# Two-stage cross attention: the first pair's v taken from row totals that VectorE turns and a DMA moves, in place of four small products of TensorE

## The chip, the core and the metric

The kernel runs on one core of one Trainium2 chip. The metric is the device time of one execution in microseconds; the time given for a kernel is the median of its runs.

## What is computed

```python
# stage one: x (16, 256, 512), ctx (16, 256, 512)
q = einsum('blh,oh->blo', x, w_q)
k = einsum('bsh,oh->bso', ctx, w_k)
v = einsum('bsh,oh->bso', ctx, w_v)
probs = softmax(einsum('blh,bsh->bls', q, k) / sqrt(512))
x = x + alpha * einsum('blh,oh->blo', einsum('bls,bsh->blh', probs, v), w_o)
# stage two: x (16, 256, 512) as (b, c, n), x_2 = ctx as (b, c, n)
g_x     = (g_w @ x_2 + g_b).transpose(0, 2, 1)
theta_x = (theta_w @ x + theta_b).transpose(0, 2, 1)
phi_x   = phi_w @ x_2 + phi_b
y = ((theta_x @ phi_x) / 512 @ g_x).transpose(0, 2, 1)
wy = w_w @ y + w_b
out = bn_gamma * (wy - bn_mean) * rsqrt(bn_var + 1e-5) + bn_beta + x
```

Stage two has no softmax, so the kernel multiplies in another order. It needs, for each batch, phi_x times the transposed context. The bias g_b enters through one number for each of the 128 inner channels: the sum of phi_x over its 512 columns. That vector of 128 numbers for each batch is what the kernel calls `v`. It equals phi_w times the row totals of the context (256 totals for each batch) plus 512 times phi_b.

## The kernel before

The 16 batches go in 8 pairs. `pair(0, first=True)` is written out, pairs 1 to 6 are a loop on every engine, pair 7 is written out again. In front of pair 0 stands a setup: it multiplies the weights (w_k with w_q into `qk`, w_v with w_o into `ov`, g_w with w_w into `wg`), and makes the first tiles of the first pair.

Every float32 factor is split into a high and a low half (`_hi`, made by ScalarE in the helper `hi`, L634; `_lo`, made by VectorE in the helper `lo`, L892). A product of float32 tiles is then three products of TensorE: `product`, L363 to L370. The order of the work is written out by hand on each engine, and semaphores join the engines. SyncE issues most of the DMAs, ScalarE's queue a few.

Names that the change and the prediction speak of:

- `c_sums` (L656): ScalarE runs over `c_raw`, the context of a pair, and leaves the row totals in `c_sum`: partition p, one column for each batch and each of its two row tiles. It costs four activations with an accumulator for each pair.
- `send_sums` (L663) and `fetch_sums` (L668): both issued by ScalarE. The first stores `c_sum` to the DRAM tensor `sums_moved`, two values (8 bytes) for each partition and batch. The second reads it back, broadcast to all 128 partitions, into columns of the tile `row` (`sum_rows`).
- `weigh_sums` (L998) on VectorE multiplies `sum_rows` by `phi_rows` (phi_w, one row for each partition), and `v_sums` (L768) on ScalarE adds each row up into `v`. Pairs 1 to 7 get their `v` in this way; the store and the fetch stand in the pair ahead.
- `first_v` (L449): pair 0 gets its `v` from TensorE. ScalarE makes the high half of the totals (`sum_sides`, L703), VectorE the low half (L976), TensorE multiplies phi_w by them in four products with a moving side of 4 or 2 columns, and VectorE adds two columns and the bias (L1167, L1169).
- `t1_rows` (L1082) on VectorE uses `v`; its result goes into `t1`, and TensorE waits for `t1_made` ahead of `gram_rows(1, 0)` in pair 0.
- `gram_rows` (L436), `gram_squares`, `gram_close`, `gram_part`: context times transposed context; its lower blocks travel through DRAM. `phi_gram` (L445) multiplies phi_w by it; in pair 0 TensorE waits there for `gram_lo`.
- `theta_rows` (L491) waits for the low half of x1 (`x1_lo`), and `delta` for the low half of `vo` and of `pT`.

```python
            def first_v():
                pe.wait_ge(sums_lo, 1)
                for k in range(KS):
                    pe.matmul(bank[FIRST_V_BANK][:, 0:4], phi_w[0][:, k], sum_sides[:, k].rearrange("p h b -> p (h b)"),
                              start=(k == 0), stop=False)
```

## Time and profile before

| | |
|---|---|
| time, median of 3 runs | 388.9 us (388.58 to 389.62) |
| time of the profiled execution | 388.78 us |
| span of the profiled execution | 386.8 us |
| granted clock of TensorE over the span | 0.999 |
| instructions | 5571 |
| VectorE busy | 310.8 us, 80% |
| ScalarE busy | 206.0 us, 53% |
| packets of ScalarE's DMA queue (q10) | 3632, 2.77 MB, 2.5% of the 16 engines' span |
| share of TensorE in the chain that ended last | 97% |

The span is the time from the first to the last instruction on the core; the device time of the same execution is 1.98 us longer. TensorE's matmuls overlap in the records: each of 512 columns is shown with some 0.39 us, while one starts every 0.23 us. So a wait of TensorE is read from the starts in a timeline, and not from its busy time alone.

### The profile page before, as it was taken

The numbers are of one execution on the slowest core, as the hardware profiler recorded it, in microseconds if no ns is written. First come the engines' busy times: TensorE is split into PE (matmuls) and PEld (weight loads), VectorE is DVE, ScalarE is ACT, GpSimd is POOL, SyncE is SP. The second block draws the span as 40 slices with busy tenths as digits, with TensorE's granted clock in tenths as the row PEclk, the third lists the DMA queues.
The fourth block names the chain that finished last, engine by engine and source line by source line (L and its number), as shares of the span: only waits on it lengthen the run. The fifth ranks groups of instructions, "written<-read, shape, count | busy, mean of one in ns | idle before, by whom it ended". The sixth has DMA issues, their size and how long they took to land.

```text
span 386.8 us, 5571 instructions
## 1 busy us (share of the span) xinstructions
PE 381.8 (99%) x1783; PEld 319.5 (83%) x1783; DVE 310.8 (80%) x590; ACT 206.0 (53%) x440; POOL 0.4 (0%) x5
## 2 busy tenths in 40 slices
PE   8999999999999999999999999999999999999995
PEld 5888888888888888888888888888888888888885
DVE  5899778887699777986798967986788876986786
ACT  4477668433664267543665258452665347552553
POOL 0000000000000000000000000000000000000000
PEclk9999999999999999999999999999999999999999
DMA  8985741476386646856356655865496664044423
GB/s 248 379 319 198 266 128 54 150 283 233 110 212 193 240 139 214 166 190 216 107 178 206 216 169 177 217 186 192 122 204 177 211 190 136 19 117 153 145 83 108
DMA packets 59563, 70.11 MB, mean 181 GB/s; under 512 B 6688, under 2 KB 49568, under 8 KB 56480
## 3 DMA queue, kind: packets, MB, share of 16 engines
q1 hardware_dynamic: 55920, 67.20, 56.0%
q10 hardware_dynamic: 3632, 2.77, 2.5%
q8 instruction: 6, 0.10, 0.1%
q14 instruction: 5, 0.04, 0.0%
HBM read 51.06 MB, written 18.89 MB: 181 GB/s over the span
## 4 chain that ended last, share of the span: by engine, by line
PE 97%; DMA 1%; DVE 1%; ACT 0%; issue 0%; SPq 0%
PE bank L367 24%; PE bank L368 23%; PE bank L369 23%; PE bank L421 8%; PE bank L440 7%; PE bank L407 5%; PE bank L429 4%; PE bank L472 2%; PE bank L476 1%; DMA xb<-w_k 1%; DVE xb L1152 0%; DVE xb L1147 0%; PE bank L393 0%; ACT theta_hi L634 0%; ACT t_sides L634 0%
## 5 line engine op out<-in xcount | busy, mean ns | idle before, releaser
L367 PE MATMUL bank<-ov_hi,c_sides 128*128 128x512 f32 x128 | 50.0, 391 | 0.0
L368 PE MATMUL bank<-c_sides,qk_hi 128*128 128x512 f32 x128 | 49.9, 390 | 0.0
L369 PE MATMUL bank<-c_sides,qk_lo 128*128 128x512 f32 x128 | 49.9, 390 | 0.0
L368 PE MATMUL bank<-ov_lo,c_sides 128*128 128x512 f32 x128 | 49.9, 390 | 0.0
L367 PE MATMUL bank<-c_sides,qk_hi 128*128 128x512 f32 x128 | 49.8, 389 | 0.0
L369 PE MATMUL bank<-ov_hi,c_sides 128*128 128x512 f32 x128 | 49.8, 389 | 0.0
L634 ACT ACTIVATE t_sides<-bank 128x512 fp32r<-128x512 f32 x32 | 19.0, 593 | 36.9 <-PE bank L369 36.9
L421 PE MATMUL bank<-t_sides,xT_hi 128*128 128x512 f32 x128 | 31.9, 391 | 0.0
L634 ACT ACTIVATE probs<-bank 128x512 f32<-128x512 f32 x16 | 9.4, 586 | 37.9 <-PE bank L429 37.9
L892 DVE TENSOR_TENSOR t_sides<-bank,t_sides 128x512 fp32r<-128x512 f32 x32 | 22.0, 687 | 8.5 <-ACT t_sides L634 8.5
L634 ACT ACTIVATE x_hi<-xb 128x512 fp32r<-128x512 f32 x32 | 19.9, 630 | 16.4 <-DVE xb L1072 16.2
L369 PEld LDWEIGHTS bank<-ov_hi,c_sides 128*128 128x128 f32 x128 | 24.0, 188 | 5.1
L369 PEld LDWEIGHTS bank<-c_sides,qk_lo 128*128 128x128 f32 x128 | 24.0, 188 | 5.1
L367 PEld LDWEIGHTS bank<-ov_hi,c_sides 128*128 128x128 f32 x128 | 24.1, 188 | 4.8
L368 PEld LDWEIGHTS bank<-c_sides,qk_hi 128*128 128x128 f32 x128 | 24.0, 188 | 4.8
L367 PEld LDWEIGHTS bank<-c_sides,qk_hi 128*128 128x128 f32 x128 | 24.0, 188 | 4.8
L368 PEld LDWEIGHTS bank<-ov_lo,c_sides 128*128 128x128 f32 x128 | 24.1, 188 | 4.7
L440 PE MATMUL bank<-c_sides 128*128 128x384 f32 (+1 forms) x128 | 27.4, 364 | 0.0
L421 PEld LDWEIGHTS bank<-t_sides,xT_hi 128*128 128x128 f32 x128 | 23.5, 188 | 4.5
L440 PEld LDWEIGHTS bank<-c_sides 128*128 128x128 f32 x128 | 23.5, 188 | 3.1
L367 PE MATMUL bank<-vo_hi,pT_hi 128*128 128x512 f32 x64 | 25.0, 391 | 0.0
L737 ACT ACTIVATE probs<-probs,neg_max 128x256 f32<-128x256 f32 x32 | 16.0, 502 | 16.7 <-DVE neg_max L1020 16.7
(157 smaller groups left out, 815.4 us busy)
## 6 DMA issues: line engine op xcount, KB each, us to landing
cT_raw<-ctx_t SPq DMA_DIRECT2D x8, 1024.0 KB, 8.0
xT_raw<-x_t SPq DMA_DIRECT2D x8, 1024.0 KB, 5.1
c_raw<-ctx_n SPq DMA_DIRECT2D x8, 1024.0 KB, 8.1
xb<-x SPq DMA_DIRECT2D x16, 512.0 KB, 4.1
out<-xb SPq DMA_DIRECT2D x14, 512.0 KB, 2.8
gram_moved<-gram_blocks SPq DMA_DIRECT2D x16, 256.0 KB, 2.7
gram_blocks<-gram_moved SPq DMA_DIRECT2D x64, 64.0 KB, 1.9
moved<-blocks SPq DMA_DIRECT2D x16, 256.0 KB, 2.3
```

The lines of the kernel that those rows point to most:

```text
L367: pe.matmul(dst, ahi, bhi, start=(k == 0), stop=False)
L368: pe.matmul(dst, ahi, blo, start=False, stop=False)
L369: mm = pe.matmul(dst, alo, bhi, start=False, stop=(k == k_tiles - 1))
L407: mm = pe.matmul(bank[KH * n + m][:], lhs[a][:, k, tile(m)], rhs[b][:, k, :], start=(k == 0 and a == b), stop=(k == KH - 1 and a == 1))
L421: mm = pe.matmul(banks[:, SCORE_BANK[b]][:, lt], xT[0][:, b, k, tile(lt)], t_sides[:, k, b].rearrange("p h s -> p (h s)"), start=(k == 0), ...
L429: mm = pe.matmul(banks[:, SCORE_BANK[b]][:, lt, 0:S], xT[1][:, b, k, tile(lt)], tT[0][:, k, b], start=False, stop=(stop and k == KH - 1))
L440: mm = pe.matmul(bank[GRAM_BANK[b][i]][:, i * P:], cT[0][:, k, b, tile(i)], c_sides[:, k, b].rearrange("p h s -> p (h s)")[:, i * P:], sta ...
L472: pe.matmul(banks[:, t1_banks][:, n], u[0][:, 2 * b + k], wg_sides[:, k].rearrange("p h l -> p (h l)"), start=(k == 0), stop=False)
L476: mm = pe.matmul(banks[:, t1_banks][:, n, 0:L], u[1][:, 2 * b + k], wg[0][:, k], start=False, stop=(k == KS - 1))
L634: act.activation(dst, src, ACT.Identity, **more).then_inc(made, 1)
L737: e = act.activation(probs[:, b, lt], probs[:, b, lt], ACT.Exp, bias=neg_max[:, b, lt:lt + 1], scale=SCALE, accum_out=row_sum[:, b, lt:lt ...
L892: dve.tensor_tensor(parts[1][at], src, parts[0][at].bitcast(F32), ALU.subtract).then_inc(made, 1)
```

## The change

1. `first_v`, the two halves of `sum_sides`, `phi_h` and the two additions that opened its bank are gone.
2. `c_sum` becomes a tile of 128 x 32, cleared once by GpSimd. VectorE transposes it in 32 x 32 blocks into `c_sum_blocks` (`turn_sums`), once in the setup and once in each of the pairs 0 to 6. `send_sums` stores that tile, 128 bytes from each partition; `fetch_sums` reads 4 runs of 512 bytes for each partition, where it read one of 2048. `phi_n` has its columns in the new order, and `weigh_sums` and `v_sums` walk over four pieces of 64 columns.
3. In the setup ScalarE now issues a store of the first pair's totals and a fetch of them. In pair 0 VectorE's `weigh_sums` and ScalarE's `v_sums` are added.
4. In pair 0 `send_sums` stands behind `x1_part(0, .)`; in the loop it stands where it stood, and waits for `sums_turned`.
5. TensorE no longer waits for `v_made` in pair 0.

```diff
-        sum_sides = sb("sum_sides", [P, KS, 2, 2], F32R)
-        c_sum = sb("c_sum", [P, 2 * KS])
-        phi_h = sb("phi_h", [P, 1])
-        sums_moved = nc.dram_tensor("sums_moved", [2, P, KS], F32).ap()
-        sum_rows = row[:, ROW_GAMMA:ROW_GAMMA + 2 * S].rearrange("p (b s) -> p b s", b=2)
+        c_sum = sb("c_sum", [P, SQUARE])
+        c_sum_blocks = sb("c_sum_blocks", [P, SQUARE])
+        sums_moved = nc.dram_tensor("sums_moved", [BLOCKS, SQUARE * SQUARE], F32).ap()
+        sums_in = row[:, ROW_GAMMA:ROW_GAMMA + 2 * S].rearrange("p (q n) -> p q n", q=BLOCKS)
+        sum_rows = sums_in.rearrange("p q (b n) -> p b q n", b=2)
@@ -542,7 +531,6 @@
                     phi_gram(FIRST_PHI_BANK)
-                    first_v()
                     pe.wait_ge(wg_lo, 1)
...
                     pe.wait_ge(phi_turned, p + 1)
-                    pe.wait_ge(v_made, 2)
@@ -661,14 +648,13 @@
             def send_sums(count):
-                act.wait_ge(c_summed, count)
-                act.dma_start(sums_moved.rearrange("b p k -> p b k"),
-                              c_sum[:].rearrange("p (b k) -> p b k", b=2)).then_inc(sums_stored, 16)
+                act.wait_ge(sums_turned, count)
+                act.dma_start(sums_moved.rearrange("q (j i) -> (q j) i", j=SQUARE),
+                              c_sum_blocks[:]).then_inc(sums_stored, 16)
             def fetch_sums(count):
                 act.wait_ge(sums_stored, count)
-                act.dma_start(row[:, ROW_GAMMA:ROW_GAMMA + 2 * S],
-                              sums_moved.rearrange("b p k -> (b p k)").partition_broadcast(P)).then_inc(sums_loaded, 16)
+                act.dma_start(sums_in, sums_moved[:, 0:2 * KS * SQUARE].partition_broadcast(P)).then_inc(sums_loaded, 16)
...
+            act.wait_ge(ones_made, 2)
             c_sums(16)
-            act.wait_ge(c_summed, 4)
-            hi(sum_sides[:, :, 0], c_sum[:].rearrange("p (b k) -> p k b", b=2), sums_hi)
             tT_part(1, 2)
+            send_sums(1)
...
-            for b in range(2):
-                gram_part(b, KS * (b + 1))
+            gram_part(0, KS)
+            act.wait_ge(bn_step, 6)
+            fetch_sums(16)
+            gram_part(1, 2 * KS)
...
                 if first:
                     u_part()
+                    v_sums()
                     c_sums(loads[32])
-                send_sums(four[8])
+                else:
+                    send_sums(pairs_done[2])
                 for lt in range(KL):
                     x1_part(0, lt)
                 if first:
+                    send_sums(2)
                     t1_part(0)
                     t1_part(1)
@@ -960,21 +950,26 @@
+            def turn_sums(summed, stored_bytes=None):
+                dve.wait_ge(c_summed, summed)
+                if stored_bytes is not None:
+                    dve.wait_ge(sums_stored, stored_bytes)
+                dve.transpose(c_sum_blocks[:], c_sum[:]).then_inc(sums_turned, 1)
+
+            turn_sums(4)
             tT_part(1, 2)
...
                 if first:
                     phi_squares(1, FIRST_PHI_BANK)
-                    dve.wait_ge(first_v_done, 1)
-                    dve.tensor_scalar(v[:], bank[FIRST_V_BANK][:, 0:2], phi_h[:], None, ALU.add).then_inc(first_v_opened, 1)
-                    dve.wait_ge(first_v_opened, 1)
-                    dve.tensor_tensor(v[:], bank[FIRST_V_BANK][:, 2:4], v[:], ALU.add).then_inc(v_made, 2)
...
                 if first:
+                    weigh_sums(16)
                     pT_part(1)
...
                 if first:
                     u_rows()
+                else:
+                    turn_sums(summed[8], loads[16])
                 for half in range(2):
                     cT_part(half, two[3 + half])
...
                 x1_rows(0)
+                if first:
+                    turn_sums(8, 16)
...
             pool.memset(g_bias[:], 1.0).then_inc(ones_made, 1)
+            pool.memset(c_sum[:], 0.0).then_inc(ones_made, 1)
```

TensorE at the end of pair 0's `phi_gram`, before (L367 to L369 are `product`, L452 and L455 `first_v`):

```order
L367 MATMUL bank<-gram_hi,phi_w_hi 128x512
L368 MATMUL bank<-gram_lo,phi_w_hi 128x512
L369 MATMUL bank<-gram_hi,phi_w_lo 128x512
L452 MATMUL bank<-sum_sides,phi_w_hi 128x4 [waits c_sums_lo_made]
L452 MATMUL bank<-sum_sides,phi_w_hi 128x4
L455 MATMUL bank<-sum_sides,phi_w_lo 128x2 x2
L367 MATMUL bank<-ov_hi,c_sides 128x512 [waits wg_bias_made,wg_lo_made]
L368 MATMUL bank<-ov_lo,c_sides 128x512
```

and changed:

```order
L366 MATMUL bank<-gram_hi,phi_w_hi 128x512
L367 MATMUL bank<-gram_lo,phi_w_hi 128x512
L368 MATMUL bank<-gram_hi,phi_w_lo 128x512
L366 MATMUL bank<-ov_hi,c_sides 128x512 [waits wg_bias_made,wg_lo_made]
L367 MATMUL bank<-ov_lo,c_sides 128x512
```

The four small products are gone and nothing takes their place; the rest of TensorE's order is the same.

ScalarE in the setup, from the totals on, before:

```order
L660 ACTIVATE c_raw,c_sum<-c_raw 128x512 x3
L634 ACTIVATE sum_sides<-c_sum 128x2x2 [waits c_summed]
L634 ACTIVATE t_sides<-bank 128x2x256 [waits tT_done]
L634 ACTIVATE t_hi<-phi_blocks 128x256 [waits ww_scaled]
L634 ACTIVATE u_hi<-g_bias 128x128 [waits g_bias_made]
L634 ACTIVATE t_sides<-bank 128x2x256 [waits tT_done] x2
L719 ACT_TABLE_LOAD
L719 ACTIVATE neg_max<-std_col 128x2
L634 ACTIVATE gram_hi<-gram_raw 128x2x256 [waits gram_made] x2
```

and changed:

```order
L647 ACTIVATE c_raw,c_sum<-c_raw 128x512 x3
L621 ACTIVATE t_sides<-bank 128x2x256 [waits tT_done]
L652 DMA sums_moved<-c_sum_blocks 128x32 [waits c_sums_turned]
L621 ACTIVATE t_hi<-phi_blocks 128x256 [waits ww_scaled]
L621 ACTIVATE u_hi<-g_bias 128x128 [waits g_bias_made]
L621 ACTIVATE t_sides<-bank 128x2x256 [waits tT_done] x2
L676 ACT_TABLE_LOAD
L676 ACTIVATE neg_max<-std_col 128x2
L621 ACTIVATE gram_hi<-gram_raw 128x2x256 [waits gram_made]
L657 DMA row<-sums_moved 128x4x128 [waits c_sums_stored,bn_step]
L621 ACTIVATE gram_hi<-gram_raw 128x2x256 [waits gram_made]
```

The store comes in behind the second tile of `t_sides`, the fetch between the two halves of `gram_hi`, with a wait for the store.

VectorE in pair 0, from the first low half of `pT` on, changed (L1036 is `pT_part`, L996 `weigh_sums`, L958 `turn_sums`, L1084 `t1_rows`):

```order
L1036 TENSOR_TENSOR pT_lo<-probs,pT_hi 128x512 [waits pT_hi_made]
L996 TENSOR_TENSOR row<-row,phi_rows 128x4x64 [waits c_sums_loaded]
L996 TENSOR_TENSOR row<-row,phi_rows 128x4x64
L1036 TENSOR_TENSOR pT_lo<-probs,pT_hi 128x512 [waits pT_hi_made]
...
L1069 SCALAR_TENSOR_TENSOR xb<-bank,inv_sum,xb 128x512 [waits delta_done]
L958 STREAM_TRANSPOSE c_sum_blocks<-c_sum 128x32 [waits c_sums_stored,c_summed]
L1084 SCALAR_TENSOR_TENSOR blocks<-wg_bias,v,bank 128x256 [waits v_made,t1_done,wg_bias_made]
```

Before, the rows L996 and L958 were not there, and the two rows of `pT_lo` stood together.

## Rows read from the trace of the kernel before

**Rows 1.** The page: busy time of TensorE, share of the span, instructions.
```profile
PE 381.8 (99%) x1783; PEld 319.5 (83%) x1783; DVE 310.8 (80%) x590; ACT 206.0 (53%) x440; POOL 0.4 (0%) x5
```

**Rows 2.** Waits of TensorE, all of them: us in total, times, longest.
```profile
PE bank L382 <- PEq L1280: 0.8, 1, 0.8
PE bank L393 <- ACT t_sides L634: 0.2, 1, 0.2
```

**Rows 3.** Timeline, TensorE around the small products: start us, us, engine, line, operation.
```profile
47.40 0.39 PE L367 MATMUL bank<-gram_hi,phi_w_hi 128*128 128x512 f32 x1
...
48.76 0.28 PE L452 MATMUL bank<-sum_sides,phi_w_hi 128*128 128x4 f32 x2
...
49.12 0.49 PE L367 MATMUL bank<-ov_hi,c_sides 128*128 128x512 f32 x1
...
49.45 0.40 PE L368 MATMUL bank<-ov_lo,c_sides 128*128 128x512 f32 x1
```

**Rows 4.** Timeline, TensorE in pair 1, at its second delta.
```profile
108.29 0.39 PE L369 MATMUL bank<-vo_hi,pT_lo 128*128 128x512 f32 x1
108.55 0.47 PE L367 MATMUL bank<-vo_hi,pT_hi 128*128 128x512 f32 x1
108.86 0.39 PE L368 MATMUL bank<-vo_lo,pT_hi 128*128 128x512 f32 x1
```

**Rows 5.** Timeline, VectorE: one of its small operations.
```profile
52.09 0.16 DVE L1169 TENSOR_TENSOR v<-bank,v 128x2 f32<-128x2 f32 x1
```

**Rows 6.** Timeline, VectorE in the setup, with its idle time ahead and what ended it.
```profile
37.35 0.69 DVE L892 TENSOR_TENSOR t_sides<-bank,t_sides 128x512 fp32r<-128x512 f32 x1 [0.59 <-ACT t_sides L634]
...
45.68 0.69 DVE L892 TENSOR_TENSOR gram_lo<-gram_raw,gram_hi 128x512 fp32r<-128x512 f32 x1 [0.70 <-ACT gram_hi L634]
```

**Rows 7.** Timeline, ScalarE in the setup.
```profile
39.02 0.42 ACT L634 ACTIVATE t_hi<-phi_blocks 128x256 fp32r<-128x256 f32 x1 [1.69 <-DVE phi_blocks L970]
...
45.02 0.63 ACT L634 ACTIVATE gram_hi<-gram_raw 128x512 fp32r<-128x512 f32 x1 [1.43 <-DVE gram_raw L991]
```

**Rows 8.** Timeline, DMA issues of SyncE: a load in the setup, one in pair 0.
```profile
40.87 0.43 SPq L223 DMA_DIRECT2D xT_raw<-x_t  x1
...
65.66 0.36 SPq L226 DMA_DIRECT2D cT_raw<-ctx_t  x1
```

**Rows 9.** Line L665 (`send_sums`), all seven: issue to landing.
```profile
DMA to landing us min/median/max: 2.8/7.2/7.8
```

**Rows 10.** The same line, pair 0's alone: its issue and its landing.
```profile
L665 ACTq DMA_DIRECT2D sums_moved<-c_sum x1: 388/388/388, 65.9 to 65.9; - x1
...
DMA to landing us min/median/max: 6.1/6.1/6.1
```

**Rows 11.** Timeline, VectorE in pair 0, and pair 1's `weigh_sums`.
```profile
59.81 0.69 DVE L1039 TENSOR_TENSOR pT_lo<-probs,pT_hi 128x512 fp32r<-128x512 f32 x1 [1.04 <-ACT pT_hi L634]
...
66.98 0.87 DVE L1087 SCALAR_TENSOR_TENSOR blocks<-wg_bias,v,bank 128x256 f32<-128x256 f32 x2
...
72.94 0.77 DVE L927 STREAM_TRANSPOSE gram_blocks<-gram_raw 128x256 f32<-128x256 f32 x2 [0.90 <-ACT gram_raw L634]
...
75.75 1.28 DVE L892 TENSOR_TENSOR x_lo<-xb,x_hi 128x512 fp32r<-128x512 f32 x2
...
88.81 0.75 DVE L1001 TENSOR_TENSOR row<-row,phi_rows 128x256 f32<-128x256 f32 x2
```

**Rows 12.** Timeline, ScalarE: end of pair 0's totals; one activation of pair 1's `v_sums`.
```profile
65.69 0.19 ACT L660 ACTIVATION_READ_ACCUMULATOR c_raw<-c_raw 128x1 f32 x1
...
92.44 0.50 ACT L771 ACTIVATE row<-row,phi_bias 128x256 f32<-128x256 f32 x1
```

**Rows 13.** Timeline, TensorE at pair 0's second `theta_rows`.
```profile
77.06 0.39 PE L367 MATMUL bank<-x_hi,theta_w_hi 128*128 128x512 f32 x1
```

**Rows 14.** Timeline of pair 1: VectorE's low half of `cT`, and TensorE's `gram_rows` behind it.
```profile
108.59 2.36 DVE L892 TENSOR_TENSOR c_sides<-cT_raw,c_sides 128x1024 fp32r<-128x1024 f32 x2
...
111.39 1.98 PE L440 MATMUL bank<-c_sides 128*128 128x512 f32 x8
```

More of the change, by code:

```diff
@@ L133, in two_stage_cross_attention @@
         VO_BANK = [[2, 3], [6, 7]]
-        PHI_BANK, FIRST_PHI_BANK, FIRST_V_BANK = 2, 6, 7
+        PHI_BANK, FIRST_PHI_BANK = 2, 6
         DELTA_BANK = [[2, 3], [4, 5]]
@@ L168, in two_stage_cross_attention @@
         sums_weighted = sem("c_sums_weighted")
-        sums_hi, sums_lo = sem("c_sums_hi_made"), sem("c_sums_lo_made")
-        first_v_done, first_v_opened = sem("first_v_done"), sem("first_v_opened")
+        sums_turned = sem("c_sums_turned")
         var_made, std_made = sem("var_made"), sem("std_made")
@@ L447, in phi_gram @@
                         lambda k: cut(gram, every, k), KS).then_inc(phi_done, 1)
-            def first_v():
-                pe.wait_ge(sums_lo, 1)
-                for k in range(KS):
-                    pe.matmul(bank[FIRST_V_BANK][:, 0:4], phi_w[0][:, k], sum_sides[:, k].rearrange("p h b -> p (h b)"),
-                              start=(k == 0), stop=False)
-                for k in range(KS):
-                    mm = pe.matmul(bank[FIRST_V_BANK][:, 0:2], phi_w[1][:, k], sum_sides[:, k, 0], start=False,
-                                   stop=(k == KS - 1))
-                mm.then_inc(first_v_done, 1)
             def w_g_bias():
@@ L719, in _ @@
             act.activation(neg_max[:, 0], std_col[:], ACT.Exp)
-            for b in range(2):
-                gram_part(b, KS * (b + 1))
+            gram_part(0, KS)
+            act.wait_ge(bn_step, 6)
+            fetch_sums(16)
+            gram_part(1, 2 * KS)
             def pair(p, first=False, last=False):
                 loads = counts(act, p, 16, [16, 32])
-                landed, pairs_done = counts(act, p, 16 * BLOCKS, [16 * BLOCKS]), counts(act, p, 1, [1])
+                landed, pairs_done = counts(act, p, 16 * BLOCKS, [16 * BLOCKS]), counts(act, p, 1, [1, 2])
                 two, four = counts(act, p, 2, [-1, 0, 1, 2, 3]), counts(act, p, 4, range(-2, 9))
@@ L768, in v_sums @@
                 def v_sums():
-                    act.wait_ge(sums_weighted, two[0])
+                    act.wait_ge(sums_weighted, two[2])
                     for b in range(2):
@@ L871, in pair @@
                     act.wait_ge(v_made, two[2])
-                    fetch_sums(loads[16])
+                    fetch_sums(loads[32])
                 for b in range(2):
@@ L875, in pair @@
                 if first:
-                    act.wait_ge(bn_step, 9)
-                    fetch_sums(loads[16])
+                    act.wait_ge(v_made, 2)
+                    fetch_sums(32)
                 tT_part(2, four[7])
@@ L1000, in weigh_sums @@
                 for b in range(2):
-                    dve.tensor_tensor(sum_rows[:, b], sum_rows[:, b], phi_rows[:], ALU.mult).then_inc(sums_weighted, 1)
+                    dve.tensor_tensor(sum_rows[:, b], sum_rows[:, b], phi_rows[:].rearrange("p (q n) -> p q n", q=BLOCKS),
+                                      ALU.mult).then_inc(sums_weighted, 1)
             for b in range(2):
@@ L1008, in pair @@
                 loads = counts(dve, p, 16, [0, 16])
+                summed = counts(dve, p, 4, [8])
                 landed = counts(dve, p, 16 * BLOCKS, [16 * BLOCKS, 32 * BLOCKS])
@@ L1155, in pair @@
                 if not first:
-                    weigh_sums(loads[0])
+                    weigh_sums(loads[16])
                 row_maxima(0)
@@ L1269 @@
         "g_w": a[l1 + "g_w"],
-        "phi_n": a[l1 + "phi_w"].reshape(CI, KS, P).transpose(0, 2, 1).reshape(CI, S),
+        "phi_n": a[l1 + "phi_w"].reshape(CI, KS, BLOCKS, SQUARE).transpose(0, 2, 1, 3).reshape(CI, S),
         "phi_w_t": a[l1 + "phi_w"].T,
```

14 lines of the change are left out of this document (5 added, 9 removed).

## Prediction

> **What bounds the kernel now.** I read the page first. TensorE is busy for 381.8 of 386.8 us, VectorE for 310.8 and ScalarE for 206.0 [rows 1]. Then the waits of TensorE: there are two, 0.8 and 0.2 us, both in the first microseconds [rows 2]. A busy share can hide a wait, since matmuls overlap in the records, so I read the starts in the timeline next. From 47.40 to 48.76 six products of 512 columns start in 1.36 us, one each 0.227 us [rows 3]. That pitch holds nearly everywhere. The exceptions that matter are two: the four small products of pair 0 [rows 3], and one place in pair 1, where the starts 108.29, 108.55 and 108.86 are 0.26 and 0.31 us apart, some 0.12 us over the pitch [rows 4]. So the time is the sum of TensorE's pitches. An edit is worth what it takes out of TensorE's queue or what it makes TensorE wait; work on VectorE, ScalarE or a DMA counts only once its cover is used up. I therefore took each new instruction to the place where it stands and looked for the idle time ahead of it and for TensorE's next wait.
>
> **What the change takes from TensorE.** The first small product starts at 48.76, where the next product of 512 columns would have started. The product L367 starts at 49.12 and L368 at 49.45 [rows 3]. Without the small ones L367 would start at 48.76 and L368 one pitch on, at 48.99. The saving is 49.45 - 48.99 = 0.46 us: 0.36 for the four products themselves (0.09 each) and 0.10 for the pitch behind them, which is 0.33 where it is 0.23 elsewhere.
>
> The Trainium skill ("TensorE: Matmul & The Clock Gate", section Back-to-back issue gap) gives a moving side of 1 to 64 columns an issue gap of about 60 cycles, or 25 ns. By that rule the four products would be worth 0.10 us and the sum would be -0.1 us; the starts of this trace say otherwise.
>
> The wait of TensorE for `v_made` goes too. It cost nothing: no wait stands there [rows 2].
>
> **What it adds in the setup.** VectorE gets one transpose of 32 columns for each partition. No row shows that size. Below, a small operation takes 0.16 us [rows 5]; above, two transposes of 256 columns take 0.77 us, so 0.39 each (at 72.94) [rows 11]. I take 0.2, since 32 columns are nearer to the small one. It stands ahead of a row with 0.59 us of idle time [rows 6], so it costs nothing; without that cover it would cost 0.2 to 0.4 us of VectorE. ScalarE's store stands ahead of a row with 1.69 us of idle time [rows 7], and a DMA issue takes about 0.4 us [rows 8]: nothing. ScalarE's fetch stands between the halves of `gram_hi`, where the second half follows 1.43 us of idle time and starts at 45.02 [rows 7]: nothing, if the store has landed by then. The store is issued at about 37.1 us by my count (VectorE's transpose just ahead of its row at 37.35 [rows 6]), and the seven stores of before took 2.8 to 7.8 us to land [rows 9], so it lands between 39.9 and 44.9. VectorE's low half ends at 45.68 + 0.69 = 46.37 and TensorE's `phi_gram` starts at 47.40 [rows 3, 6], so the second half may slip by 1.03 us before TensorE feels it. With the issue of the fetch in front, the store has until 45.02 + 1.03 - 0.35 = 45.7. Both ends of the landing are inside. A change of packet size, 8 bytes to 128, I cost at nothing from there.
>
> **What it adds in pair 0.** VectorE's `weigh_sums`: its two operations take 0.75 us in pair 1 and stand ahead of a row with 1.04 us of idle time [rows 11]; covered, with 0.3 left. The four pieces of 64 columns in place of one run may make them and `v_sums` slower; 0.3 us is there for that. ScalarE's `v_sums`: two activations of 0.50 us [rows 12] ahead of the row totals, which ended at 65.88 [rows 12] and now end at 66.9. VectorE's second transpose waits for these totals. It comes ahead of `t1_rows`, which started at 66.98 [rows 11], so VectorE is late there by 0.1 to 0.5 us; I take 0.25. The next idle time of VectorE is the 0.90 us ahead of 72.94 [rows 11]. TensorE will be 0.46 us earlier, and so will what that idle time waits for, which leaves 0.44: enough for 0.25, and for most of the range. Behind it the low half of x1's first tile is ready at 75.75 + 0.64 = 76.39, against TensorE's `theta_rows` at 77.06 [rows 11, 13], another 0.67 us. Together 1.1 us stand against a lateness of at most 0.5. Cost: nothing.
>
> **What it adds in the loop.** One transpose a pair, between the last low half of `vo` and that of `cT`. The tightest place is pair 1: VectorE ends `cT` at 108.59 + 2.36 = 110.95, TensorE's `gram_rows` start at 111.39 [rows 14], so 0.44 us cover a transpose of 0.16 to 0.39. Cost nothing, up to 0.1 at the upper end with a semaphore's way. VectorE's new waits there are for totals and for a store of the pair before, both long done. ScalarE's store now waits for the transpose, ahead of `x1_part`, which itself waits for VectorE; nothing.
>
> **The sum.** 388.78 us for the profiled execution, minus 0.46, plus 0 (0 to 0.1), is 388.3. The profiled execution lies 0.12 us below the median of the runs, 388.9; against the median I forecast 388.4, a gain of 0.12%. A measurement of this kernel can tell about 0.3%, or 1.17 us, from no change, so this counts as the same.
>
> **Rivals.**
>
> A, *the gain is lost in pair 1's wait.* TensorE already waits some 0.12 us at its second delta there [rows 4]. If what it waits for does not move up with TensorE (a DMA's trip or a stall of SyncE that keeps its time), the 0.46 us turn into wait and the time is 388.9. For it: the wait is there, in pair 1 alone. Against it: the chain in front (scores, exponentials, the squares' trip through DRAM) begins with TensorE's own products, and moves with them. If the wait went altogether the time would be 388.3.
>
> B, *the setup's store lands late, and the kernel gets slower.* The mechanism is ScalarE's wait for its own store between the halves of `gram_hi`. It decides from a landing at 45.7 us on; each microsecond behind that is one of TensorE. In pair 0 the store of 2 KB, issued at 65.9 right behind SyncE's load of 1 MB (65.66), took 6.1 us against 2.8 for the quickest [rows 8 to 10]: a small store behind a large load lands late. In the setup SyncE's two loads of 1 MB start at 40.87 [rows 8]. If the store gets behind them and needs 7.8 us from there, it lands at 48.7. TensorE then waits 48.7 - 45.7 = 3.0 us, and the time is 388.4 + 3.0 = 391.4, 0.6% slower. Against it: 3.8 us lie between the store's issue and that load.
>
> The Trainium skill ("DMA: Bandwidth & Descriptors", section Queues, rings and completion order) says that each DMA engine takes turns, packet by packet, between the queue rows that have work. By that rule ScalarE's store would not stand behind SyncE's load at all, and B could not happen; the landing of 6.1 us in pair 0 speaks for some standing in line, so B keeps a small chance.
>
> C, *VectorE's cover in pair 0 or pair 1 is too thin.* If the transposes, the four-piece operations or the new waits cost twice what I take, TensorE waits 0.1 to 0.4 us at `theta_rows` or at pair 1's `gram_rows`, and the time is 388.5 to 388.8. Against it are the 1.1 and 0.44 us counted above.
>
> **Chances.** My forecast 0.65, A 0.15, C 0.07, B 0.06, and 0.07 for what no row shows. A and C stay within 0.3%. Slower by over 0.3%: B with a little of the unknown, 0.08. Faster by over 0.3%: nothing in the trace is worth 1.2 us; 0.05 is for the unknown. The same: 0.87. The range: at the lower end the forecast with the lowest run's distance from the median (0.3) and pair 1's wait gone (0.12), so 387.9; at the upper end A at 388.9 with half of the distance of the highest run (0.7), so 389.3. That leaves out B and most of the unknown.
>
> **What the profile would show.** Right: from the last product of `phi_gram` on, TensorE starts a product each 0.227 us with nothing between; all starts of pair 0 behind it are 0.46 us earlier; the list of TensorE's waits is as short as before; the transpose takes about 0.2 us; the setup's store lands before 44 us, and the second `gram_hi` starts at 45.0. Wrong, with A: pair 1's delta starts as late as before, with a gap in front of it. Wrong, with B: `gram_hi` starts past 46 us behind a DMA, and TensorE has a wait at `phi_gram`. Wrong, with C: a gap at 76.6 us or ahead of pair 1's `gram_rows`. The forecast as a whole is wrong if TensorE shows new waits of over half a microsecond in sum.

## The result and the profile after

The changed kernel takes 389.88 us in the median of 22 runs (389.38 to 391.72). The kernel before, run between them on the same chip, takes 389.24 us in 22 runs (388.34 to 390.0). The ratio is 1.0018, with a 95% interval of 1.0011 to 1.0025. That is a loss of 0.7 us: above zero by the whole interval, and below the 0.3% that the prediction set as the bound of "the same". The forecast was 388.4 us with a range up to 389.3: "the same" is right, the sign is wrong, and the time lies above the range. (The kernel before is itself 0.34 us above the three-run median that the forecast started from.)

The profiled execution of the changed kernel took 389.7 us, with a span of 387.5 against 386.8 before. From its page, the busy time of each engine, and from part 3 the queue of ScalarE's transfers (packets, MB, share of the DMA engines):

```profile
PE 382.0 (99%) x1779; PEld 319.7 (83%) x1779; DVE 312.0 (81%) x596; ACT 206.3 (53%) x443; POOL 0.5 (0%) x6
...
q10 hardware_dynamic: 6096, 3.15, 3.7%
```

Against [rows 1], busy times hardly moved. The waits of TensorE in the changed kernel (line, what released it, us in total, times, longest), to be held against [rows 2], did:

```profile
PE bank L381 <- PEq L1279: 0.8, 1, 0.8
PE bank L366 <- DVE vo_lo L883: 0.8, 1, 0.8
```

The second line is new. TensorE's timeline shows where it stands, and also the place of the edit:

```profile
48.84 0.40 PE L368 MATMUL bank<-gram_hi,phi_w_lo 128*128 128x512 f32 x1
49.07 0.40 PE L366 MATMUL bank<-ov_hi,c_sides 128*128 128x512 f32 x1
49.30 0.40 PE L367 MATMUL bank<-ov_lo,c_sides 128*128 128x512 f32 x1
...
108.13 0.39 PE L368 MATMUL bank<-vo_hi,pT_lo 128*128 128x512 f32 x1
109.29 0.47 PE L366 MATMUL bank<-vo_hi,pT_hi 128*128 128x512 f32 x1 [0.77 <-DVE vo_lo L883]
109.59 0.39 PE L367 MATMUL bank<-vo_lo,pT_hi 128*128 128x512 f32 x1
```

At 48.84 to 49.30 the products of 512 columns follow each other at 0.23 us with nothing between: the four small products are gone, with the long pitch behind them [rows 3]. At 108.13 comes the second delta of pair 1. It should have started at 108.36 and started at 109.29, with a second pitch of 0.30: 0.93 + 0.07, 1.0 us of wait, where before it was 0.12 [rows 4].

**The account.** TensorE's first `gram_rows` starts at 26.85, 0.30 us later than before. In the other thirteen profiles of this study it starts anywhere from 26.33 to 27.17, in kernels of both kinds, so this is scatter of the head and not the change. Then: +0.30 of head, -0.46 for the small products, +0.89 at pair 1's delta (1.01 against 0.12). The sum is +0.73, and the spans differ by 0.72. Without the head it is +0.43; the larger part of what the medians show (0.64).

So a step that was to cost nothing costs twice what the edit saves. The chain of waits of the changed kernel tells which (start, us, what), followed back from the delta that waited:

```profile
87.36 3.86 DMA phi_moved<-phi_blocks
...
92.56 1.83 DMA phi_blocks<-phi_moved
...
94.94 0.61 DVE phi_blocks L1053 x2
95.55 0.63 DVE blocks L1023
96.20 2.29 DMA moved<-blocks
...
99.33 1.56 SPq L242
...
101.50 2.32 DMA moved<-blocks
...
105.13 2.08 DMA probs<-moved
...
108.50 0.69 DVE vo_lo L883
...
109.29 0.47 PE bank L366
```

It begins with the trip of phi's squares through DRAM (store `phi_moved`, fetch `phi_blocks`). VectorE adds them in `u_rows` (L1053), and only behind that does it turn the squares of the scores (L1023), whose own trip through DRAM feeds `pT`, and `pT` feeds `vo`. The DMA issues of SyncE in the kernel before and in the changed one show how much each step moved:

```profile
87.53 0.38 SPq L238 DMA_DIRECT2D phi_moved<-phi_blocks  x1
...
90.07 1.84 SPq L243 DMA_DIRECT2D phi_blocks<-phi_moved  x4
...
95.60 0.39 SPq L238 DMA_DIRECT2D moved<-blocks  x1
```

```profile
87.36 0.38 SPq L237 DMA_DIRECT2D phi_moved<-phi_blocks  x1
...
91.24 1.75 SPq L242 DMA_DIRECT2D phi_blocks<-phi_moved  x4
...
96.20 0.38 SPq L237 DMA_DIRECT2D moved<-blocks  x1
```

The store of phi's squares is issued 0.17 us earlier than before, as TensorE is (0.30 - 0.46). The fetch behind it starts 1.17 us later: the store took 3.9 us to land where it took 2.5. The first store of the scores' squares is then 0.60 us later, 0.76 against TensorE. VectorE's idle time in the changed kernel names the same transfer:

```profile
94.41 1.14 DVE L1053 SCALAR_TENSOR_TENSOR phi_blocks<-row,c_sum,phi_blocks 128x128 f32<-128x128 f32 x4 [0.87 <-DMA phi_blocks<-phi_moved]
```

What delays a store of SyncE's queue that the change does not touch? The store is issued at 87.36, and 5.4 us ahead of it, at 82.0, ScalarE issues the fetch of the row totals. In pair 0 it took 7.1 us to land (to 89.1) where it took 5.8 before (82.2 to 88.0), with the 1 MB loads of SyncE's queue around it. Its landing in the later pairs, where less is beside it, in the kernel before:

```profile
L670 ACTq DMA_DIRECT2D row<-sums_moved x6: 331/331/337, 123.1 to 344.3; - x6
...
DMA to landing us min/median/max: 3.0/3.3/3.4
```

and changed kernel:

```profile
L657 ACTq DMA_DIRECT2D row<-sums_moved x6: 382/382/382, 123.8 to 345.0; - x6
...
DMA to landing us min/median/max: 4.7/6.6/6.7
```

The same 256 KB, from DRAM to all 128 partitions, take twice as long. Over the window 80 to 97 us ScalarE's queue holds this share of the DMA engines (packets, MB, share), before:

```profile
q10 hardware_dynamic: 144, 0.26, 4.0%
```

and changed:

```profile
q10 hardware_dynamic: 528, 0.26, 11.7%
```

The packets of pair 0 show how the fetch and the store meet. From 82 to 85 us both kernels move SyncE's packets alone: the fetch, issued at 82, moves nothing while the 1 MB loads do. From 87 to 88 us the changed kernel moves the fetch alone; this is all of that microsecond (packets, MB, share; a packet counts where it starts, so a share can pass 100%):

```profile
q10 hardware_dynamic: 160, 0.08, 108.8%
```

The kernel of experiment 6, whose fetch is quick again, moves in the same microsecond:

```profile
q1 hardware_dynamic: 100, 0.41, 99.4%
q10 hardware_dynamic: 50, 0.02, 7.3%
```

(q1 is SyncE's queue.) Between the fetch and `phi_moved` SyncE has also issued a store of 512 KB of `out`, at 85.25; it lands after 5.2 us for 3.8 before. In all thirteen profiles in which the fetch stands at this place, SyncE issues the fetch of `phi_blocks`, for which `phi_moved` must have landed, 1.9 to 2.2 us after ScalarE's fetch has landed. In the changed kernel's later pairs `phi_moved` is issued 8.8 us or more behind the fetch, which has landed by then, and TensorE does not wait. That is why a fetch that is slow in every pair costs in pair 1 alone.

Two things about the fetch are new. It moves four pieces of 512 bytes for each partition in place of one run of 2048 bytes, and the four pieces lie 4096 bytes apart in DRAM (`sums_moved` is now 4 rows of 1024 numbers). The experiments tell these apart.

### The profile page after: what moved, and what is told of

Read it like the earlier page. It is cut to its first block, busy times and chain, and to the rows that moved or that the text cites. A ratio compares the mean times of both kernels' runs of the same rounds, so it can differ in the third digit from the quotient of the medians.

```text
span 387.5 us, 5582 instructions
## 1 busy us (share of the span) xinstructions
PE 382.0 (99%) x1779; PEld 319.7 (83%) x1779; DVE 312.0 (81%) x596; ACT 206.3 (53%) x443; POOL 0.5 (0%) x6
## 4 chain that ended last, share of the span: by engine, by line
PE 92%; DMA 3%; DVE 1%; SPq 1%; issue 1%; ACT 0%; DVEq 0%
PE bank L366 22%; PE bank L367 22%; PE bank L368 22%; PE bank L439 7%; PE bank L420 7%; PE bank L406 5%; PE bank L428 3%; PE bank L461 2%; SPq L242 1%; DMA moved<-blocks 1%; DMA phi_moved<-phi_blocks 1%; PE bank L381 1%; PE bank L465 1%; DMA probs<-moved 1%; DMA phi_blocks<-phi_moved 0%
## 5 line engine op out<-in xcount | busy, mean ns | idle before, releaser
L367 PE MATMUL bank<-c_sides,qk_hi 128*128 128x512 f32 x128 | 49.9, 390 | 0.0
L367 PE MATMUL bank<-ov_lo,c_sides 128*128 128x512 f32 x128 | 49.9, 390 | 0.0
L367 PEld LDWEIGHTS bank<-ov_lo,c_sides 128*128 128x128 f32 x128 | 24.1, 188 | 4.8
L367 PEld LDWEIGHTS bank<-c_sides,qk_hi 128*128 128x128 f32 x128 | 24.0, 188 | 4.8
```

The lines of the kernel that those rows point to most:

```text
L367: pe.matmul(dst, ahi, blo, start=False, stop=False)
```

## The experiments

Twelve experiments in three groups, each run beside the kernel before on the same chip. The median of the kernel before was 389.09, 389.32 and 389.91 us in the three groups, so a time is held against that of its own group. Experiments 7, 11 and 12 are one execution each, and are read for the landing of the fetch. "The wait at pair 1" is always the lateness of the second delta's first two starts against a pitch of 0.23: 0.12 us before, 1.0 in the changed kernel.

### 1. The totals in one run (first group)

```diff
-sums_moved = nc.dram_tensor("sums_moved", [BLOCKS, SQUARE * SQUARE], F32).ap()
+sums_moved = nc.dram_tensor("sums_moved", [SQUARE, BLOCKS * SQUARE], F32).ap()
...
-act.dma_start(sums_moved.rearrange("q (j i) -> (q j) i", j=SQUARE), c_sum_blocks[:])
+act.dma_start(sums_moved.rearrange("j (q i) -> q j i", q=BLOCKS), c_sum_blocks[:])
...
-act.dma_start(sums_in, sums_moved[:, 0:2 * KS * SQUARE].partition_broadcast(P))
+act.dma_start(sums_in, sums_moved[0:2 * KS].rearrange("j n -> (j n)").partition_broadcast(P))
```

The store keeps its 128-byte runs; the fetch reads 2048 bytes in a row, and `weigh_sums` works on one run again, with the weights in their plain order.

> The changed kernel, but the turned totals are laid out in DRAM so that the fetch reads one run of 2048 bytes for each partition, as before the change, and not four of 512; the store keeps its 128 pieces of 128 bytes. Theory T (the four-piece fetch of pair 0 holds up the store of the phi squares behind it, and that makes TensorE wait at pair 1's second delta): ScalarE's fetch of pair 0 lands by 88.0 us again, phi_moved lands about 2.5 us after its issue and not 3.9, the wait at pair 1's second delta falls from 1.0 us to 0.1 to 0.4 us, and the time falls by 0.6 to 0.9 us against the changed kernel, to 0.2 to 0.4 us under the kernel before (ratio 0.999). Rival R (the fetch that is new in the setup, or the work added on VectorE and ScalarE in pair 0, delays the chain): the wait of 1.0 us stays and the time stays 0.6 us over the kernel before (ratio 1.0018).

Measured: 388.82 us (388.57 to 389.17, 11 runs), a ratio of 0.9991 [0.9982, 1.0000]. The landing of the fetch in the later pairs, and SyncE's issues, in its trace:

```profile
DMA to landing us min/median/max: 3.0/3.1/3.3
```

```profile
87.16 0.38 SPq L237 DMA_DIRECT2D phi_moved<-phi_blocks  x1
...
89.52 1.79 SPq L242 DMA_DIRECT2D phi_blocks<-phi_moved  x4
...
95.24 0.38 SPq L237 DMA_DIRECT2D moved<-blocks  x1
```

The fetch is quick again. The time from the issue of `phi_moved` to that of `phi_blocks` is 2.36 us, where it was 3.88 with the change and 2.54 before; the squares' store is back at its place, and the wait at pair 1 is 0.20 us. Everything else of the change is still there, transposes and all. The store is the one other thing that this edit touches: its issue on ScalarE in pair 0 takes 0.56 us for 0.33, at 67.1 us, long before `phi_moved` at 87.16, and experiments 6 to 12 have the same. So nearly all of the added wait comes from how the fetch reads.

### 2. The kernel before with a fetch into four pieces (first group)

```diff
+PIECE = P + 16
...
+row = sb("row", [P, ROW_GAMMA + BLOCKS * PIECE])
...
+sum_pieces = row[:, ROW_GAMMA:ROW_GAMMA + BLOCKS * PIECE].rearrange("p (q n) -> p q n", q=BLOCKS)[:, :, 0:P]
+sum_rows = sum_pieces.rearrange("p (b h) n -> p b h n", b=2)
...
-act.dma_start(row[:, ROW_GAMMA:ROW_GAMMA + 2 * S],
-              sums_moved.rearrange("b p k -> (b p k)").partition_broadcast(P)).then_inc(sums_loaded, 16)
+act.dma_start(sum_pieces,
+              sums_moved.rearrange("b p k -> (b p k)").rearrange("(q n) -> q n", q=BLOCKS)
+              .partition_broadcast(P)).then_inc(sums_loaded, 16)
```

The source stays one run; only the four 512-byte pieces in SBUF lie apart.

> The kernel before with one edit: the fetch of the totals writes four pieces of 512 bytes in each partition, with a gap between them, where it wrote 2048 bytes at once. Everything else, first_v too, stays. Theory T: the wait at pair 1's second delta grows from 0.1 us to 0.6 to 1.0 us (TensorE comes 0.46 us later than in the changed kernel, so a little of it is absorbed) and the time is 0.4 to 0.9 us over the kernel before (ratio 1.001 to 1.0023). Rival R: nothing moves, ratio 1.000.

Measured: 389.44 us (388.76 to 390.19), a ratio of 1.0006 [0.9996, 1.0016]; the wait at pair 1 is 0.21 us. The landing in the later pairs:

```profile
DMA to landing us min/median/max: 3.2/3.4/3.7
```

I had expected the slow fetch and the wait to appear here. They did not: 512-byte packets alone cost 0.1 us of landing. The theory that the size of the pieces makes the fetch slow has fallen; what was left was their distance in DRAM.

### 3. The squares ahead of phi's rows (first group)

```diff
+                turn_squares(0)
                 if not first:
                     u_rows()
-                turn_squares(0)
```

The changed kernel; in pairs 1 and on, VectorE turns the first squares of the scores before it waits for phi's.

> The changed kernel with one edit: in pairs 1 to 7 VectorE transposes the first batch's probabilities ahead of u_rows, which waits for the phi blocks from DRAM. Theory T says that the delay reaches TensorE through this order (phi blocks late, u_rows late, transpose late, squares of pT late): with the transpose first, the store of the squares in pair 1 is issued at about 95.5 us and not 96.2, the wait at pair 1's second delta falls from 1.0 us to 0.1 to 0.4 us although the phi blocks are as late as ever, and the time falls by 0.6 to 0.9 us (ratio 0.999). A rival T2, that SyncE itself is late because its fetch of the phi blocks stands ahead of the store of the squares in its queue: the store of the squares does not move, and the wait stays at 1.0 us.

Measured: 389.41 us (388.5 to 390.92, 12 runs), a ratio of 1.0006 [0.9993, 1.0019]. The wait at pair 1 fell from 1.0 to 0.69 us only. SyncE's issues:

```profile
93.75 0.37 SPq L231 DMA_DIRECT2D xb<-x  x1
...
96.19 0.38 SPq L237 DMA_DIRECT2D moved<-blocks  x1
...
100.83 0.39 SPq L237 DMA_DIRECT2D moved<-blocks  x1
```

TensorE is 0.75 us late in this profile from its head on, so the store at 96.19 stands for 95.45 in the changed kernel's time, 0.75 us earlier than there. The order was part of the path, then. But that store landed 2.8 us after its issue instead of 2.3, beside SyncE's load of x (issued at 93.75, landed 4.2 us later), and the second one took 3.4 instead of 2.3. The load of x had landed before the second one was issued, so what held that one is not shown. The edit gets something back and loses part of it in the two stores. By its time it can't be told from the kernel before, and the reading stays partial.

### 4. Pair 0's fetch issued earlier (first group)

```diff
+                if first:
+                    act.wait_ge(v_made, 2)
+                    fetch_sums(32)
                 x1_part(1, 0)
...
-                if first:
-                    act.wait_ge(v_made, 2)
-                    fetch_sums(32)
```

The changed kernel; the slow fetch now runs at 71.9 us instead of 82.0, to be done before `phi_moved`.

> The changed kernel with one edit: pair 0's fetch of the totals, in four pieces still, is issued at about 72 us, ahead of SyncE's two loads of 1 MB at 79.6 and 80.1, where it was issued at 82.0 behind them. Theory T: the queue is clear when the phi blocks are stored at 87.4, they land 2.5 us later, the wait at pair 1's second delta falls to 0.1 to 0.4 us, ratio to the kernel before 0.999. If the pieces cost by themselves wherever the fetch stands, or if the setup's fetch is what matters (rival R), ratio 1.0018 as for the change. It could also hold up the squares of the context's product, stored at 73.6: then a new wait shows ahead of phi_gram in pair 0, at 85 us.

Measured: 391.38 us (391.1 to 392.06, 6 runs), a ratio of 1.0055 [1.0043, 1.0068], the slowest of the first group. Its waits of TensorE:

```profile
PE bank L366 <- DVE gram_lo L883: 1.1, 1, 1.1
PE bank L366 <- DVE vo_lo L883: 1.0, 1, 1.0
```

The fetch's packets moved from 72.9 to 76.9 us, just where the squares of the Gram matrix make their trip. Their two stores took 4.1 and 5.0 us to land where both took 2.3 before, and TensorE waited 1.1 us for `gram_lo`. SyncE's loads of 1 MB moved back to 82.8 and 83.3 us, so `phi_moved` was not early either: its fetch followed 3.25 us behind its issue (89.58, 92.83). The time and the wait at pair 1 came out against the expectation; the wait for `gram_lo` is the one that it had named as possible. So the slow fetch delays the trip of another store too, where it is issued beside one. The wait of 1.0 us at pair 1 is no test of the fetch here, since the late loads now stand in front of `phi_moved`.

### 5. The changed kernel once more (second group)

No edit; it is the reference of this group, beside the kernel before.

> The changed kernel once more, on the chip of the three runs beside it, so that they can be set against it and not only against the kernel before. If the wait at pair 1's second delta is the cause of the loss it is there again at 0.8 to 1.1 us, the fetches in the loop land 6.5 to 6.7 us after their issue, phi_moved in pair 0 takes 3.5 to 4 us, and the ratio is 1.0015 to 1.0025.

Measured: 389.97 us (389.31 to 391.32), a ratio of 1.0018 [1.0007, 1.0028], the first result again. The wait at pair 1 is 0.99 + 0.08 us. In this profile 0.62 us more are lost when TensorE waits for phi's low half at `w_g_phi` (98.87). That is the late trip of phi's squares again, reaching TensorE by its shorter way. In this profile ScalarE issues the fetch only at 83.8, after a longer wait for VectorE; it lands at 89.9, and `phi_moved` takes 3.7 us. In the first profile that wait did not show; if it comes in part of the executions, it would fill the gap between 0.43 us by the account and 0.64 by the medians. That is an inference from two profiles.

### 6. The same layout with rows 4352 bytes apart (second group)

```diff
-sums_moved = nc.dram_tensor("sums_moved", [BLOCKS, SQUARE * SQUARE], F32).ap()
+sums_moved = nc.dram_tensor("sums_moved", [BLOCKS, SQUARE * SQUARE + 64], F32).ap()
-act.dma_start(sums_moved.rearrange("q (j i) -> (q j) i", j=SQUARE), c_sum_blocks[:])
+act.dma_start(sums_moved[:, 0:SQUARE * SQUARE].rearrange("q (j i) -> q j i", j=SQUARE), c_sum_blocks[:])
```

The changed kernel with 64 unused numbers behind each row of the DRAM buffer. Number and size of the fetch's pieces stay the same.

> The changed kernel with one edit: the four rows of the turned totals in DRAM are 4352 bytes apart and not 4096. Still 512 packets of 512 bytes. The fetch of the kernel before with four pieces out of one contiguous run of 2048 bytes landed in 3.4 us, the changed kernel's in 6.6, so it is where the pieces lie in DRAM that costs. Theory P (the step of exactly 4096 bytes): the fetch lands in 3.2 to 3.8 us in the loop, phi_moved takes 2.5 us, the wait falls to 0.1 to 0.4 us, ratio 0.999. Rival Q (any layout that isn't one contiguous run costs, whatever the step): 6.4 to 6.8 us, the wait stays, ratio 1.0018.

Measured: 388.91 us (388.09 to 390.25, 11 runs), a ratio of 0.9993 [0.9981, 1.0004] to the kernel before, and 1.06 us below the changed kernel's median in the same group (0.4 to 1.8 when the runs of both are resampled). Landing in the later pairs:

```profile
DMA to landing us min/median/max: 3.2/3.3/3.4
```

and TensorE at pair 1's second delta:

```profile
107.94 0.40 PE L368 MATMUL bank<-vo_hi,pT_lo 128*128 128x512 f32 x1
108.17 0.40 PE L366 MATMUL bank<-vo_hi,pT_hi 128*128 128x512 f32 x1
108.41 0.39 PE L367 MATMUL bank<-vo_lo,pT_hi 128*128 128x512 f32 x1
```

256 bytes of padding take the fetch from 6.6 to 3.3 us and the wait from 1.0 us to none. With the size and the number of the pieces unchanged, their distance in DRAM is the cause.

### 7 and 11. Rows 640 and 2048 bytes apart (second and third group, one execution each)

```diff
-sums_moved = nc.dram_tensor("sums_moved", [SQUARE, BLOCKS * SQUARE], F32).ap()
+sums_moved = nc.dram_tensor("sums_moved", [SQUARE, 160], F32).ap()
...
-act.dma_start(sums_moved.rearrange("j (q i) -> q j i", q=BLOCKS), c_sum_blocks[:])
+act.dma_start(sums_moved[:, 0:P].rearrange("j (q i) -> q j i", q=BLOCKS), c_sum_blocks[:])
...
-act.dma_start(sums_in, sums_moved[0:2 * KS].rearrange("j n -> (j n)").partition_broadcast(P))
+act.dma_start(sums_in.rearrange("p (j n) -> p j n", j=2 * KS),
+              sums_moved[0:2 * KS, 0:P].partition_broadcast(P))
```

Both start from experiment 1; number 11 has 512 in place of 160.

> The kernel with one contiguous run for the fetch, but its four rows of 512 bytes 640 bytes apart in DRAM; a look at the fetch alone. Theory P: it lands in 3.2 to 3.8 us, as the four pieces out of a contiguous run did. Rival Q: 6.4 to 6.8 us.

> A look at the fetch with its four rows of 512 bytes 2048 bytes apart, which is half of the step that costs. If the cost belongs to a step of a whole multiple of 4096: it lands in 3.2 to 3.5 us. If any large power of two costs, half of the effect or all of it: 4.5 to 6.6 us.

Measured: 388.58 us with a landing of 3.3 us (median) at 640 bytes, and 389.53 with 3.2 at 2048. Neither distance slows the fetch. Their waits at pair 1 are 0.47 and 0.58 us, more than the 0.12 of before with the fetch as quick as there. That part is not the fetch's; the paragraphs on what stays open come back to it.

### 8. One run and the squares first (second group)

The edits of experiments 1 and 3 together.

> Both edits that helped: the fetch in one run of 2048 bytes, and VectorE's transpose of the first batch's probabilities ahead of u_rows in pairs 1 to 7. If what is left of the wait at pair 1's second delta (0.2 us) is the order on VectorE, it goes, and the time is 0.1 to 0.2 us under that of the one-run kernel: ratio 0.9986 to 0.999. If it is the slow fetch issue of SyncE (1.5 us where the others take 0.43, at 99 us in both kernels), moving the transpose up by 1.1 us still takes it away, since the whole chain behind it moves. The rival: the store of the squares moves up into SyncE's load of x and lands later by what it was issued earlier, as in the run with the four-piece fetch; then nothing changes (ratio 0.999).

Measured: 389.24 us (388.56 to 390.27), a ratio of 0.9999 [0.9989, 1.0008]; the wait at pair 1 is 0.57 us, more than in experiment 1. The first store of squares is back at 2.3 us, so its way is clear. The second one, at 99.58, landed 3.7 us after its issue began, and the issue alone took 1.74 us where it takes 0.38 elsewhere. The load of x, issued at 91.58 and landed 3.8 us later, was over, so the rival that the expectation names is not what is seen. The times do not tell the two orders apart: the ratio of experiment 1 to the kernel before, 0.9991, lies within this one's interval. Nothing here speaks for the new order.

### 9 and 10. The padded kernel again, and with the small products put back (third group)

Number 9 is experiment 6 once more. Number 10 adds to it, behind pair 0's `phi_gram`, four products of TensorE of 4, 4, 2 and 2 columns whose result nobody reads, in the place of the removed ones:

```diff
+for half, n in ((0, 4), (1, 2)):
+    for k in range(KS):
+        pe.matmul(bank[7][:, 0:n], phi_w[half][:, k], phi_w[0][:, k, 0:n],
+                  start=(half == 0 and k == 0), stop=(half == 1 and k == KS - 1))
```

> The changed kernel with its four rows 4352 bytes apart, once more, as what the next run is set against on the same chip. By the theory it gains the 0.46 us of the four small products and loses nothing: ratio to the kernel before 0.9988 (0.998 to 0.9995), no wait of over 0.4 us at pair 1's second delta.

> The kernel with rows 4352 bytes apart, with four products of 4, 4, 2 and 2 columns put back behind pair 0's phi_gram. They multiply parts of phi_w and nobody reads their result; v is still made by the DMA way. By the timeline of before they cost 0.46 us: the first product of values starts 0.36 us late and the one behind it a further 0.10, and the time is 0.3 to 0.6 us over that of the run without them. A rival, that the issue floor of a product is what they cost (four times 25 ns): 0.1 us.

Measured: number 9 took 388.86 us (388.57 to 389.88, 12 runs), a ratio of 0.9960 [0.9941, 0.9978] to a kernel before that spread more in this group than in the others (389.2 to 392.75). Number 10 took 389.44 (388.67 to 390.38), a ratio of 0.9982 [0.9963, 1.0001]. Between the two lie 0.58 us (0.2 to 1.0 when the runs of both are resampled). TensorE's timeline in number 10:

```profile
49.32 0.28 PE L536 MATMUL bank<-phi_w_hi 128*128 128x4 f32 x2
49.46 0.36 PE L536 MATMUL bank<-phi_w_hi,phi_w_lo 128*128 128x2 f32 x2
49.69 0.49 PE L366 MATMUL bank<-ov_hi,c_sides 128*128 128x512 f32 x1
50.01 0.40 PE L367 MATMUL bank<-ov_lo,c_sides 128*128 128x512 f32 x1
```

From 49.32 to 50.01 are 0.69 us, of which one pitch of 0.23 would be there anyway: 0.46, the prediction's first term, by 0.37 for the products and 0.09 behind them. The Trainium skill ("TensorE: Matmul & The Clock Gate", section Back-to-back issue gap) gives an issue gap of about 25 ns for such a product; an estimate from it is 0.10 us for the four. This trace has nearly four times that, 0.37.

### 12. Rows 8192 bytes apart (third group, one execution)

As number 11, with 2048 numbers to a row.

> A look at the fetch with its four rows 8192 bytes apart. If the cost belongs to a step of a whole multiple of 4096 (all four rows meet in one place): 6.4 to 6.8 us or more. If it belongs to 4096 alone: 3.2 to 3.5 us.

Measured: 402.64 us. Landing of the fetch in the later pairs, and TensorE's waits:

```profile
DMA to landing us min/median/max: 7.7/9.5/9.7
```

```profile
PE bank L461 <- DVE u_lo L1058: 10.1, 6, 4.3
```

Now the fetch takes 9.5 us, longer than the 8.8 us in front of `phi_moved` in the later pairs. `phi_moved` takes 8.6 us in front of pair 1 and 5.1 to 6.2 us in the five pairs behind it, and TensorE loses 10.1 us at `w_g_phi` in six waits. So 8192 bytes are worse than 4096, and the loss reaches TensorE by the late trip of phi's squares.

The landing of the fetch in the later pairs (median of six), all with 256 KB to 128 partitions:

| pieces for each partition, distance in DRAM | kernel | landing, us |
|---|---|---|
| one of 2048 B | before; experiments 1; 8 | 3.3; 3.1; 3.2 |
| four of 512 B, in one run | experiment 2 | 3.4 |
| four, 640 B apart | 7 | 3.3 |
| four, 2048 B apart | 11 | 3.2 |
| four, 4096 B apart | changed; 3; 4; 5 | 6.6 in each |
| four, 4352 B apart | 6; 9; 10 | 3.3 in each |
| four, 8192 B apart | 12 | 9.5 |

## Why the prediction was wrong, point by point

**What bounds the kernel**: right. The time is the sum of TensorE's pitches, and the result is made of one pitch sum that shrank and one wait that grew.

**What the change takes from TensorE, 0.46 us**: right. 48.84, 49.07, 49.30 in the changed kernel; and experiment 10 puts it back for 0.46 by the trace and 0.58 by the medians.

**The setup**: right in each step. The transpose took 0.21 us, and the idle time behind it fell from 0.59 to 0.28. The store was issued at 37.18, landed after 2.1 us at 39.3, and the second half of `gram_hi` started at 45.32 after the same 1.43 us of idle, the head's 0.30 later than before. Rival B did not come up. The fetch of the setup took 7.5 us, from 43.3 to 50.8, far ahead of `weigh_sums` at 58.64.

**Pair 0's cover**: right, and C did not come up. VectorE in the changed kernel:

```profile
58.64 0.75 DVE L996 TENSOR_TENSOR row<-row,phi_rows 128x256 f32<-128x256 f32 x2
...
67.08 0.21 DVE L958 STREAM_TRANSPOSE c_sum_blocks<-c_sum 128x32 f32<-128x32 f32 x1
67.22 0.85 DVE L1084 SCALAR_TENSOR_TENSOR blocks<-wg_bias,v,bank 128x256 f32<-128x256 f32 x2
...
72.78 0.77 DVE L918 STREAM_TRANSPOSE gram_blocks<-gram_raw 128x256 f32<-128x256 f32 x2 [0.53 <-ACT gram_raw L621]
```

`weigh_sums` takes 0.75 us for four pieces, as for one run. The transpose takes 0.21, `t1_rows` starts at 67.22 for 66.98 [rows 11], which is less than the head's 0.30; I had allowed 0.25 on top. So 0.53 us of idle time are left of the 0.90 at the gram transposes [rows 11], where the forecast left 0.19. `theta_rows` starts at 76.90 against 77.06 [rows 13]: 0.46 us earlier, less the head's 0.30. **The loop's transposes** cost nothing either: in pair 1 VectorE ends `cT` at 111.68, and TensorE's `gram_rows` start at 112.13.

**The step that failed** is a term that the sum does not have: what the fetch's new form costs in the DMA engines. The prediction says "A change of packet size, 8 bytes to 128, I cost at nothing from there", which is about the store, and asks of the four pieces only whether they slow VectorE and ScalarE. It counted the fetch's issue and its reader's slack. What the fetch itself does in the DMA engines, and who stands behind it there, was never asked, though the profile of the kernel before has it: a fetch at 82.2 us, with a store of `out` at 85.45 and `phi_moved` at 87.53 behind it. The runs put these numbers in that place: in the later pairs the fetch takes 6.6 us for 3.3, in pair 0, where it matters, 7.1 for 5.8, so that it lands 1.1 us later; `phi_moved` takes 3.9 for 2.5, and TensorE pays 0.89.

**Rival A** had the right place and the wrong size. It said that pair 1's delta could keep its time while TensorE comes earlier, and bounded the loss by the gain, 0.46. Against it the prediction held that the chain in front "begins with TensorE's own products, and moves with them". One of its links does not: VectorE's `u_rows` stands ahead of the squares' transpose and waits for phi's trip through DRAM. That trip got longer, the gate moved 0.74 us back (the last `vo` half ends at 109.19 for 108.45), and TensorE came 0.16 us earlier. A rival whose gate can move needs a price for its moving, and is not bounded by the gain.

**The chances**: "the same", at 0.87, came true, but not for the reason given. The loss of 0.89 and the gain of 0.46 both happen to be smaller than the 1.17 us that count as a difference.

**The range** ended at A plus scatter, so it missed by 0.6 us. Of this 0.34 is the base: three runs gave 388.9 for a kernel whose 22 runs give 389.24. The sign that the prediction named for "wrong, with A" (the delta as late as before or later, with a gap in front of it) is the line that showed it.

**What stays open.** Why 4096 and 8192 bytes are slow, and 2048 and 4352 are not, was not taken further. The Trainium skill ("DMA: Bandwidth & Descriptors", section Latency and other measured facts) reports lower rates for copies whose rows lie 512 KiB and more apart at powers of two, and takes their cause for an inference; no run here has such distances.

The rest of the wait at pair 1 goes from none to 0.58 us in kernels with a quick fetch. By and large it goes with one slow issue: of SyncE's four fetches of the first squares (at 99.33 in the chain above), one takes far more than the 0.43 us of the others, in every profile of the list:

| kernel | longest of the four issues, us | wait at pair 1, us |
|---|---|---|
| 6 | 1.28 | none |
| 10 | 1.42 | 0.06 |
| before | 1.49 | 0.12 |
| 9 | 1.51 | 0.02 |
| 1 | 1.59 | 0.20 |
| 2 | 1.71 | 0.21 |
| 7 | 1.85 | 0.47 |
| 11 | 2.00 | 0.58 |

In the changed kernel it is 1.56 us in the first profile and 1.25 in experiment 5, with waits of 1.0 and 1.07, so it does not make the loss of this case. In experiments 3 and 8, where the squares come earlier, none of the four is slow. What stretches the issue is not known.

Whether the change, once padded, beats the kernel before was seen clearly in one group (0.9960 [0.9941, 0.9978]) and not in the other (0.9993 [0.9981, 1.0004]).

## What to carry to other kernels

When an edit changes how a transfer reads, price the transfer and not only its reader's slack: look up who issues on the other queues in the few microseconds behind it, and follow that transfer to the engine that bounds. Give DRAM scratch buffers that are read in short pieces a row distance off 4096 and 8192 bytes; 256 bytes of padding were worth 1.06 us here at 4096. In a kernel whose TensorE hardly waits, four products of 2 to 4 columns with weights of their own are worth 0.46 us, read from the starts of the products around them.

## What the runs showed of the hardware that I had not expected

- A fetch of 256 KB in 512-byte pieces for 128 partitions lands in 3.2 to 3.4 us with the pieces 512, 640, 2048 or 4352 bytes apart, in 6.6 at 4096 and in 9.5 at 8192.
- A slow fetch of ScalarE's queue holds back a store of SyncE's that is issued 5.4 us behind it: 3.9 us to land for 2.5. From 87 to 88 us only the fetch's packets move.
- A fetch of ScalarE's queue issued at 82 us, 2 us behind SyncE's loads of 1 MB, moves no packet of its own before 85 us, in the kernel before and in the changed one.
- One of four like DMA issues of SyncE took 1.25 to 2.0 us where its neighbours took 0.43, in the first pair of the loop and in twelve of the fourteen profiles.
- Stores in runs of 128 bytes land sooner than in pieces of 8 bytes: `sums_moved` in 3.8 us in the median where before it was 7.2 [rows 9]. Nothing waited for it in either kernel.
